# A two-layer graph network: second-layer matmuls in two column halves, and one-hots built tile by tile

## The chip, the cores and the metric

The kernel runs on one core of a Trainium2 chip. The metric is the device time of one execution in microseconds (us). The engines are named as the profile names them: PE is TensorE (PEld its weight loads), DVE is VectorE, ACT is ScalarE, POOL is GpSimd, SP is SyncE, which issues most of the DMAs.

## What is computed

6250 nodes and 200000 edges (sorted by target), 64 features, all float32. The reference, cut to what matters:

```python
h = relu(layernorm(x));  x = x + gcn_layer(h, src, dst)          # layer 0, untouched by the change
h = relu(layernorm(x))
message_in = concat(h[src], h[dst], edge_x)                      # 200000 x 192
message = relu(message_in @ msg_W1 + msg_b1) @ msg_W2 + msg_b2
agg = segment_sum(message, dst)
out = x + relu(concat(agg, h) @ upd_W1 + upd_b1) @ upd_W2 + upd_b2
```

## The kernel before

For the second layer `h @ W` is computed once per node for the source part (table `a`) and the target part (table `b`). What is left per edge is relu(a[src] + b[dst] + edge_x @ W_edge), summed by target. `msg_W2` is applied after the sum.

The edges are cut into 196 superblocks of 8 tiles of 128 edges. Since the edges are sorted, a superblock's targets lie in a window of 64 nodes. The tile `eo` holds per edge 64 values of `edge_x` and 64 of a one-hot of its target in that window; `wb` holds W_edge (64 rows) over the window's 64 rows of `b` (64 rows). So one matmul with 128 rows of contraction gives the edge term and the target term together, and the same one-hot serves later to sum messages into the window.

The loop (`message_passes` on DVE, the `Fori` over `passes1` on PE, here one pass) has 49 iterations of U = 4 superblocks, steps k = 0 to 3; the last two are written out. Per superblock:

- DVE `onehots_of` (through `window_onehots`, L905) compares `iota_w` with `rel` for 8 tiles in one instruction and writes the right half of `eo`. It runs three superblocks ahead.
- PE `transpose_edges` (L1692) turns 8 tiles of `eo` into PSUM, two superblocks ahead; ACT copies them to `eoT` (L1392).
- PE `edge_and_target_terms` (L1701): 8 matmuls with the stationary `eoT` tile (128x128) and the moving `wb` (128x64), one superblock ahead, into PSUM bank 2 or 3.
- DVE `add_rows` (L1137) adds the source rows and sets `added`; ACT applies `relu` (L1397); PE `sum_messages` (L1711) multiplies message tiles (128x64 stationary) with one-hots, even tiles into partitions 0 to 63, odd ones into 64 to 127; DVE `add_sums` (L1144) adds the result to `acc` at the window's base.

The source rows `a[src]` come in two ways. For 22 of the 32 tiles of an iteration POOL gathers them from DRAM (L684), one indirect DMA per tile, 8 for k = 0, 8 for k = 1, 6 for k = 3. For the other 10, in groups g = 0 and 1 of 5 tiles, PE picks them from a table held in SBUF. This path, per group:

- DVE `edges_to_slots` (L1093, L1094, L1096): a one-hot of the edge's bin (7 wide) times its source number, and a one-hot of its rank (128 wide), for 5 tiles each. The last instruction sets `ranked`. The first sets `bin_marked`, for which the third waits.
- PE `pack_slots` (L1726) waits for `ranked` and packs the source numbers into slots (5 matmuls); DVE `copy_packed` (L1101) copies them.
- PE `spread_slot_src` (L1737), ACT copy (L1405), DVE `picks` (L1109, 7 instructions of 896 elements), PE `pick_rows` (L1759, 49 matmuls, in four parts u), ACT copy (L1414).
- DVE `slots_to_edges` (L1118, 7 instructions of 640 elements), PE `return_rows` (L1773, 35 matmuls), DVE `build_rows` (L1127, three reduces).

Each engine works through an order written out by hand in `step`, and the engines meet only at semaphores:

- DVE, even k: `onehots_of` (k + 3), `add_rows` (k), `picks`, `build_rows`, `edges_to_slots` (one group on), `add_sums` (k). Odd k: `onehots_of`, `add_rows`, `copy_packed`, `slots_to_edges`, `add_sums`.
- PE, even k: `spread_slot_src`, transposes (k + 2), terms (k + 1), `return_rows`, `sum_messages` (k). Odd k: transposes, `pack_slots`, `pick_rows` u = 0 and 1, terms (k + 1), `pick_rows` u = 2 and 3, `sum_messages` (k).

An odd step's `pack_slots` thus uses the `edges_to_slots` of the even step before it. SP loads `edge_x` (two DMAs of 128 KB), source indices and the window of `b` for a superblock when `summed` and `added` of the one four before have come. POOL starts a superblock's gathers when its indices have landed (`idx_in`).

Of the kernel before, what the change touches and what calls it, by code (L numbers as in the profile page):

```python
# [20 lines left out]
def gnn_two_layers(nc: bass.Bass, x, src, dst, edge_x, l0_w, l0_b, msg_w1, msg_b1, msg_w2, msg_b2,  # L21
# [5 lines left out]
    N, D = x.shape  # L27
    E = src.shape[0]
    P = 128
# [3 lines left out]
    T = 8  # L33
    SB = T * P
    NSB = -(-E // SB)
    U = 4
# [4 lines left out]
    W = 64  # L41
# [26 lines left out]
    GTS = (5, 5)  # L68
    PT = sum(GTS)
    GOFF = (0, GTS[0])  # L70
# [6 lines left out]
    BINS = 7  # L77
# [22 lines left out]
    def wide(ap, axis, n):  # L100

        shape = list(ap.shape)
        shape[axis] = n
        return ap.broadcast_to(shape)

    ctx = ExitStack()
    with ctx:
        def sb(name, shape, dt=f32):
            return ctx.enter_context(nc.sbuf_tensor(name, shape, dt))

        def sem(name):
            return ctx.enter_context(nc.semaphore(name))
# [33 lines left out]
        pe_src, pe_bin, pe_rank, pe_slot, pe_far = (  # L146
            tmp_e[:, :, :].rearrange("p s t -> p (s t)").bitcast(fp16)[:, q * NPT:(q + 1) * NPT] for q in range(5))
# [44 lines left out]
        eo = work[:, 0:U * T * 2 * D].rearrange("p (u t d) -> p u t d", u=U, t=T)  # L192
        wb = sb("wb", [P, U, D])
        eoT = sb("eoT", [P, 2, T, P])
# [4 lines left out]
        digit16 = sb("digit16", [P, SLOTS_G], fp16)  # L199
# [44 lines left out]
        rank_oh = y_flat[:, 0:o].bitcast(fp16).rearrange("p (g t s) -> p g t s", g=2, t=GT)  # L244
        bin_src = y_flat[:, o:o + GT * BINS].bitcast(fp16).rearrange("p (g t b) -> p g t b", g=2, t=GT)
# [13 lines left out]
        psum = ctx.enter_context(nc.psum_tensor("psum", [P, 8, 512], f32))  # L259
# [63 lines left out]
        onehot = [sem(f"onehot{l}") for l in range(3)]  # L323
# [31 lines left out]
        s_tab3 = sem("s_tab3")  # L355
        s_split_v = sem("s_split_v")
        code_in = [sem("code_in0"), sem("code_in1")]
        bin_marked = sem("bin_marked")
        ranked = sem("ranked")
        packed = sem("packed")  # L360
        packed_copied = sem("packed_copied")
# [359 lines left out]
        def _(dve):  # L721
# [8 lines left out]
            V = nc.vector  # L730
# [8 lines left out]
            for c in range(0, CH, 4):  # L739
                m = min(4, CH - c)  # L740
# [24 lines left out]
            rel2 = rel[:, :, :].rearrange("p s t -> p (s t)")  # L765
# [11 lines left out]
            for c in range(0, CH, 4):  # L777
                m = min(4, CH - c)
                dve.wait_ge(s_tabT, (CH + 3) // 4 + c // 4 + 1)
                ins = V.tensor_copy(srci[:, c * P:(c + m) * P], psum[:, c // 4, 0:m * P])  # L780
# [56 lines left out]
            for g in range(CH):  # L837
                k = g % 2
# [65 lines left out]
            def window_onehots(s, out_slot):  # L904
                return V.tensor_tensor(out_slot, wide(iota_w.rearrange("p (t c) -> p t c", t=1), 1, T),  # L905
                                       wide(rel2[:, bass.ds(s * T, T)].rearrange("p (t c) -> p t c", c=1), 2, W), ALU.is_equal)
# [4 lines left out]
            for c in range(0, NB, 4):  # L911
                m = min(4, NB - c)
                dve.wait_ge(s_tr, c // 4 + 1)
                V.tensor_copy(hT[0:D, c * P:(c + m) * P], psum[0:D, (c // 4) % 2, 0:m * P]).then_inc(s_trc, 1)
            for c in range(0, NB, T):
                m = min(T, NB - c)
# [153 lines left out]
            def message_passes():  # L1070
                with dve.Fori(0, passes1) as r:

                    def onehots_of(i, k):
                        dve.wait_ge(summed[1], r * NSB + i * U + k + 1)
                        window_onehots(i * U + k, eo[:, k, :, D:2 * D]).then_inc(onehot[1], 1)

                    def pieces_of(i, g):
                        return NPIECE * (r * NIT + i) + (len(PIECES[0]) if g else 0)

                    def edges_to_slots(i, g, first=False):  # L1080
                        n = 2 * (r * NIT + i) + g
                        tiles = bass.ds(i * PT + GOFF[g], GTS[g])
                        if not first:
                            dve.wait_ge(packed, n - 1)
                        to_bin, to_rank = bin_src[:, g, 0:GTS[g], :], rank_oh[:, g, 0:GTS[g], :]

                        def each_edge(t, m):
                            return wide(t[:, tiles].rearrange("p (t c) -> p t c", c=1), 2, m)

                        def digits(m):  # L1090
                            return wide(digit16[:, 0:m].rearrange("p (t c) -> p t c", t=1), 1, GTS[g])

                        V.tensor_tensor(to_bin, digits(BINS), each_edge(pe_bin, BINS), ALU.is_equal).then_inc(bin_marked, 1)  # L1093
                        V.tensor_tensor(to_rank, digits(P), each_edge(pe_slot, P), ALU.is_equal)  # L1094
                        dve.wait_ge(bin_marked, n + 1)
                        V.tensor_tensor(to_bin, to_bin, each_edge(pe_src, BINS), ALU.mult).then_inc(ranked, 1)  # L1096

                    def copy_packed(i, g):
                        n = 2 * (r * NIT + i) + g
# [77 lines left out]
                    for k in range(1, 3):  # L1177
                        onehots_of(0, k)
# [117 lines left out]
            for c in range(0, NB, T):  # L1296
                m = min(T, NB - c)
# [153 lines left out]
        def _(pe):  # L1451
            TT = nc.tensor
# [12 lines left out]
            for c in range(0, NSB * T, 512):  # L1465
                m = min(512, NSB * T - c)
                ins = TT.matmul(psum[:, c // 512, 0:m], first_row[:, :], dstf[:, c:c + m], start=True, stop=True)
# [3 lines left out]
            for q in range(T):  # L1471
                ins = TT.matmul(psum[:, 5, 256 + q * CH:256 + (q + 1) * CH], expand[:, q, :], rawf[:, :, 0], start=True, stop=True)
# [8 lines left out]
            for half in range(2):  # L1481
                pe.wait_ge(s_edgeslot, half + 1)
                for b in range(NHALF):
                    col = 128 + half * NHALF + b
                    ins = TT.matmul(psum[:, 6, col:col + 1], edge_slot[:, b, :], ones_b[:, :], start=True, stop=True)
                ins.then_inc(s_slotcnt, 1)

            for g in range(CH):
                pe.wait_ge(s_slotoh, g + 1)
                for t in range(T):  # L1490
                    ins = TT.matmul(psum[:, 4, 0:HI], one_lo[:, g % 2, :, t], one_hi[:, g % 2, :, t],
                                    start=(g + t == 0), stop=(g + t == CH + T - 2))
                ins.then_inc(s_slothist, 1)

            with pe.If(passes > 1):
                TT.matmul(psum[:, 4, 0:HI], zeros[:, :], zeros[:, 0:HI], start=True, stop=False)
                pe.sem_inc(s_hfree, 2)
                with pe.Fori(0, NSB // 2) as i:
                    for k in range(2):
                        pe.wait_ge(s_oh, 2 * i + k + 1)  # L1500
                        for t in range(T):
                            ins = TT.matmul(psum[:, 4, 0:HI], one_lo[:, k, :, t], one_hi[:, k, :, t], start=False, stop=False)
# [21 lines left out]
            for b in range(NB):  # L1524
                c = b // 4
                if b % 4 == 0 and c >= 2:
                    pe.wait_ge(s_trc, c - 1)
                ins = TT.transpose(psum[0:D, c % 2, (b % 4) * P:(b % 4 + 1) * P], H[:, b + 1, :], ident[:, :])
# [4 lines left out]
            for b in range(NB):  # L1533
                c = b // T
                if b % T == 0 and c >= 2:
                    pe.wait_ge(s_mmc, c - 1)
                ins = TT.matmul(psum[:, 2 + c % 2, (b % T) * D:(b % T + 1) * D], hT[0:D, b * P:(b + 1) * P], w_l0[:, :],  # L1537
                                start=True, stop=True)
# [13 lines left out]
            for q in range(NCODE):  # L1552
                m = min(P, NPT - q * P)
                ins = TT.transpose(psum[0:m, 5, q * P:(q + 1) * P], code32[:, q * P:q * P + m], ident[:, :])
# [61 lines left out]
            with pe.If(passes > 1):  # L1616
                pe.sem_inc(summed[2], U)
                pe.sem_inc(acc_add[2], 2)
                with pe.Fori(0, passes) as r:
                    pe.wait_ge(counts_reset[2], r + 1)  # L1620
                    pe.sem_inc(s_turn[3], 1)
                    with pe.Fori(0, NIT) as i:
                        for k in range(U):
                            n = r * NSB + i * U + k
# [3 lines left out]
                            for t in range(T):  # L1628
                                ins = TT.matmul(psum[0:D, 6 + k % 2, 0:W], rows[:, k, t, :], onehot0[:, k, t, :],
                                                start=(t == 0), stop=(t == T - 1))  # L1630
# [3 lines left out]
            for b in range(NB):  # L1634
                c = b // T
                if b % T == 0 and c >= 4:
                    pe.wait_ge(s_gelu_in, c - 3)
                ins = TT.transpose(psum[:, c % 4, (b % T) * D:(b % T + 1) * D], acc[0:D, b * P:(b + 1) * P], ident[0:D, 0:D])
# [44 lines left out]
            with pe.Fori(0, passes1) as r:  # L1683
# [11 lines left out]
                def edge_and_target_terms(i, k):  # L1695
                    n = r * NSB + i * U + k
                    pe.wait_ge(b_in[k], 16 * (r * NIT + i + 1))
                    for t in range(T):
                        if t % 4 == 0:
                            pe.wait_ge(eoT_ready, 2 * n + t // 4 + 1)  # L1700
                        ins = TT.matmul(psum[:, 2 + k % 2, t * D:(t + 1) * D], eoT[:, k % 2, t, :], wb[:, k, :],  # L1701
                                        start=True, stop=True)
                    ins.then_inc(pre_done, 1)

                def sum_messages(i, k):
# [169 lines left out]
```

## Time and profile before

| | |
|---|---|
| time, three runs | 2358.78, 2360.42, 2361.4 us; median 2360.42 |
| profiled execution, its own time | 2360.0 us (its span) |
| instructions | 72737 |
| busy: PE, PEld, DVE, ACT, POOL | 2148.9, 1935.2, 1690.4, 1143.2, 1654.0 us |
| second layer's message loop | about 866 to 2320 us |
| L1701 (terms), PE busy | 374.4 us, 3136 records |
| L905 (one-hots, second layer), DVE busy | 135.6 us, 196 instructions |
| L1094 (rank one-hots), DVE busy | 80.1 us, 98 instructions |

How to read it: the page has the busy time of each engine and the same in 40 slices. A line of a timeline gives the start, the length, the engine, the source line and how many instructions were merged (x7); the idle time before it and what ended it stand in brackets. An instruction's length contains a tail that the next one overlaps, so the distance between starts is what one costs in a row. The chain of waits is followed back from the end of the program. "issue" is time in which the profile shows nothing that was waited for. A float32 matmul is recorded twice.

### The profile page before, as it was taken

To read this page: it belongs to the slowest core of one execution; us is meant where nothing else is said; L and a number is where in the kernel's file an instruction comes from. 1 tells how busy PE (TensorE), PEld (TensorE's weight loads), DVE (VectorE), ACT (ScalarE), POOL (GpSimd) and SP (SyncE) were. 2 spreads that over 40 slices of the span, in tenths; PEclk is the share of its full clock that TensorE was granted. 3 is DMA by queue.
4 is the path that set the end of the run, shared out by engine and by line. 5 is a ranking of instruction groups with operands and counts; after the bars stand their busy time and mean duration, and the time that the engine had idled before them with its cause. 6 is when DMAs were issued, how large, how long until landed. Compare 5 with 4: busy or idle time off the path is not lost.

```text
span 2360.0 us, 72737 instructions
## 1 busy us (share of the span) xinstructions
PE 2148.9 (91%) x23689; PEld 1935.2 (82%) x23690; DVE 1690.4 (72%) x4590; ACT 1143.2 (48%) x2411; POOL 1654.0 (70%) x1577
## 2 busy tenths in 40 slices
PE   2255999999999759999999999999999999999998
PEld 1143788887888659999999999999999999999995
DVE  8866788887888676666666666666666666666663
ACT  0003888888888644444444444444444444444442
POOL 5476777777777126777777777777777777777771
PEclk7566999999999879999999999999999999999999
DMA  2001111111112033333333333333333333333332
GB/s 74 1 1 42 26 27 27 27 27 29 27 25 28 6 86 65 73 74 74 74 74 74 74 74 74 74 74 74 74 74 74 74 74 74 74 74 74 74 75 41
DMA packets 346918, 133.36 MB, mean 57 GB/s; under 512 B 305501, under 2 KB 322755, under 8 KB 346787
## 3 DMA queue, kind: packets, MB, share of 16 engines
q1 hardware_dynamic: 298980, 82.66, 15.6%
q0 software_dynamic: 47808, 49.05, 11.1%
q8 instruction: 71, 1.16, 0.2%
q14 instruction: 59, 0.48, 0.1%
HBM read 124.04 MB, written 7.52 MB: 56 GB/s over the span
## 4 chain that ended last, share of the span: by engine, by line
PE 86%; DVE 7%; issue 3%; POOL 2%; ACT 1%; DMA 1%; DVEq 0%; SPq 0%; PEld 0%; POOLq 0%; PEldq 0%; ACTq 0%
PE psum L1759 17%; PE psum L1701 14%; PE psum L1570 12%; PE psum L1773 12%; PE psum L1602 9%; PE psum L1692 8%; PE psum L1711 5%; PE psum L1591 2%; PE psum L1737 2%; POOL rows L684 2%; PE psum L1726 1%; PE psum L1581 1%; PE psum L1537 1%; DVE work L830 1%; PE psum L1831 1%
## 5 line engine op out<-in xcount | busy, mean ns | idle before, releaser
L684 POOL DMA_INDIRECT rows<-a_rows,idx x1078 | 1110.4, 1030 | 378.9 <-issue 369.5
L1339 ACT ACTIVATE hT<-psum 128x392 bf16<-128x392 f32 x1152 | 510.6, 501 | 105.3 <-PE psum L1602 98.2
L684 POOL DMA_INDIRECT rows<-g_rows,idx x416 | 430.9, 1036 | 149.1 <-issue 125.7
L1570 PE MATMUL psum<-work,hT 128*128 128x192 bf16 x3528 | 455.0, 246 | 0.3 <-ACT hT L1339 0.3
L1759 PE MATMUL psum<-edge_index,H 128*128 128x192 bf16 x4802 | 429.2, 246 | 1.8 <-DVE H L1109 1.7
L1392 ACT ACTIVATE eoT<-psum 128x512 f32<-128x512 f32 x392 | 213.7, 602 | 404.9 <-PE psum L1692 404.8
L1759 PEld LDWEIGHTS psum<-edge_index,H 128*128 128x128 bf16 x4802 | 398.3, 99 | 3.4 <-issue 1.9
L1570 PEld LDWEIGHTS psum<-work,hT 128*128 128x128 bf16 x3528 | 323.5, 99 | 70.7 <-issue 1.0
L1602 PE MATMUL psum<-Z,one_lo 128*128 128x392 f16 x1152 | 364.8, 338 | 17.0 <-DVE Z L946 16.8
L1701 PE MATMUL psum<-wb,eoT 128*128 128x64 f32 x3136 | 374.4, 273 | 0.0
L1701 PEld LDWEIGHTS psum<-wb,eoT 128*128 128x128 f32 x3136 | 365.6, 192 | 0.1
L1414 ACT ACTIVATE Y<-psum 128x384 bf16<-128x384 f32 (+1 forms) x392 | 176.9, 451 | 365.5 <-PE psum L1759 357.0
L1773 PE MATMUL psum<-Y,Z 128*128 128x192 bf16 x3430 | 306.7, 246 | 0.9 <-ACT Y L1405 0.9
L946 DVE TENSOR_SCALAR Z<-digit,edge_index 128x392 f16<-128x392 f16 x1152 | 297.6, 328 | 0.0
L1773 PEld LDWEIGHTS psum<-Y,Z 128*128 128x128 bf16 x3430 | 294.7, 99 | 1.1 <-ACT Y L1405 1.1
L1109 DVE TENSOR_SCALAR H<-Y,node_cmp 128x896 bf16<-128x896 f16 x686 | 263.7, 452 | 7.5 <-ACT Y L1405 7.3
L1144 DVE TENSOR_TENSOR acc<-acc,psum 128x64 f32 x196 | 42.7, 218 | 311.0 <-PE psum L1711 311.0
L905 DVE TENSOR_TENSOR work<-iota_bw,rel 128x512 f32<-128x512 f32 x196 | 135.6, 692 | 118.5 <-issue 118.5
L1118 DVE TENSOR_SCALAR Z<-Z,slot_cmp 128x640 bf16<-128x640 f16 x686 | 220.2, 389 | 0.0
L1692 PE MATMUL psum<-ident,work 128*128 128x128 f32 x1568 | 212.0, 278 | 0.0
L1602 PEld LDWEIGHTS psum<-Z,one_lo 128*128 128x128 bf16 x1152 | 160.3, 145 | 38.5 <-DVE Z L946 27.9
L1692 PEld LDWEIGHTS psum<-ident,work 128*128 128x128 f32 x1568 | 168.7, 141 | 7.3
(272 smaller groups left out, 2012.6 us busy)
## 6 DMA issues: line engine op xcount, KB each, us to landing
work<-in_edge_attr_dram SPq DMA_DIRECT2D x392, 128.0 KB
rows<-a_rows,idx POOLq DMA_INDIRECT x1078
Z<-slot_code SPq DMA_DIRECT2D x98, 160.0 KB, 3.1
rows<-g_rows,idx POOLq DMA_INDIRECT x416
idx<-src_by_tile SPq DMA_DIRECT2D x200, 4.0 KB
wb<-b_rows SPq DMA_DIRECT2D x196, 16.0 KB
g_rows<-Y SPq DMA_DIRECT2D x1, 1600.0 KB, 8.9
a_rows<-Y SPq DMA_DIRECT2D x6, 256.0 KB, 2.6
```

Source lines behind the costliest of these rows:

```text
L684: pool.indirect_dma_start(out=rows[:, k, t, :], out_offset=None, in_=table, in_offset=bass.IndirectOffsetOnAxis(ap=idx[:, k, t:t + 1], axis=0)
L946: V.tensor_scalar(keys[:, g * T + t, :], key_digit[:, :], key_of[:, bass.ds(tile + t, 1)], None, ALU.is_equal).then_inc(key_ready, 1)
L1109: ins = V.tensor_scalar(pick[:, b, :], slot_src[:, :], node_cmp[:, b:b + 1], None, ALU.is_equal)
L1118: ins = V.tensor_scalar(from_slot[:, b, 0:cols], code_row[:, g, 0:cols], slot_cmp[:, b:b + 1], None, ALU.is_equal)
L1339: nc.scalar.activation(counts[:, j % 2, :, t * SLOTS:(t + 1) * SLOTS], psum[:, t % 4, 0:KEYS].rearrange("p (h m) -> p h m", m=SLOTS), ACT.Copy
L1392: nc.scalar.activation(eoT[:, k % 2, h * 4:h * 4 + 4, :], psum[:, h, :].rearrange("p (t e) -> p t e", e=P), ACT.Copy).then_inc(eoT_ready, 1)
L1570: ins = TT.matmul(psum[:, 4 + (j + 1) % 2, 0:NPART * D], counts[:, (j + 1) % 2, h, :], gtab[:, h, :, :].rearrange("p k d -> p (k d)"), sta ...
L1602: TT.matmul(psum[:, t % 4, 0:KEYS], one_lo[:, t // T, :, t % T], keys[:, t, :], start=True, stop=True).then_inc(counted, 1)
L1692: ins = TT.transpose(psum[:, h, (t % 4) * P:(t % 4 + 1) * P], eo[:, k, t, :], ident[:, :])
L1701: ins = TT.matmul(psum[:, 2 + k % 2, t * D:(t + 1) * D], eoT[:, k % 2, t, :], wb[:, k, :], start=True, stop=True)
L1759: ins = TT.matmul(psum[:, PICK_BANK[u], (b % 2) * NPART * D:(b % 2 + 1) * NPART * D], pick[:, h, b * P:(b + 1) * P], atab[:, b * BLK + h, ...
L1773: ins = TT.matmul(psum[:, bank, (t - t0) * NPART * D:(t - t0 + 1) * NPART * D], from_slot[:, b, t * P:(t + 1) * P], picked_rows[:, b, :], ...
```

## The change

- In `edge_and_target_terms` each tile's matmul becomes two, with the left and the right 64 columns of the stationary `eoT` tile (64 edges each), written to partitions 0 to 63 and 64 to 127 of the same PSUM columns. The moving operand is the same for both.
- In `onehots_of` of the second layer the one instruction for 8 tiles becomes 8 `tensor_scalar`, each comparing 64 float16 numbers (`digit16`) with the tile's column of `rel`, a per-partition scalar. The other uses of `window_onehots` stay.
- In `edges_to_slots` the three `tensor_tensor` for 5 tiles become 5 pairs of `tensor_scalar`: bin compared with `pe_bin` and multiplied with `pe_src` in one instruction, rank compared with `pe_slot`. The semaphore `bin_marked` and its wait go.

```diff
@@ DVE, onehots_of
-                        window_onehots(i * U + k, eo[:, k, :, D:2 * D]).then_inc(onehot[1], 1)
+                        for t in range(T):
+                            ins = V.tensor_scalar(eo[:, k, t, D:2 * D], digit16[:, 0:W], rel2[:, bass.ds((i * U + k) * T + t, 1)],
+                                                  None, ALU.is_equal)
+                        ins.then_inc(onehot[1], 1)
@@ DVE, edges_to_slots
-                        tiles = bass.ds(i * PT + GOFF[g], GTS[g])
                         if not first:
                             dve.wait_ge(packed, n - 1)
-                        to_bin, to_rank = bin_src[:, g, 0:GTS[g], :], rank_oh[:, g, 0:GTS[g], :]
...
-                        V.tensor_tensor(to_bin, digits(BINS), each_edge(pe_bin, BINS), ALU.is_equal).then_inc(bin_marked, 1)
-                        V.tensor_tensor(to_rank, digits(P), each_edge(pe_slot, P), ALU.is_equal)
-                        dve.wait_ge(bin_marked, n + 1)
-                        V.tensor_tensor(to_bin, to_bin, each_edge(pe_src, BINS), ALU.mult).then_inc(ranked, 1)
+                        for t in range(GTS[g]):
+                            at = bass.ds(i * PT + GOFF[g] + t, 1)
+                            V.tensor_scalar(bin_src[:, g, t, :], digit16[:, 0:BINS], pe_bin[:, at], pe_src[:, at],
+                                            ALU.is_equal, ALU.mult)
+                            ins = V.tensor_scalar(rank_oh[:, g, t, :], digit16[:, 0:P], pe_slot[:, at], None, ALU.is_equal)
+                        ins.then_inc(ranked, 1)
@@ PE, edge_and_target_terms
-                        ins = TT.matmul(psum[:, 2 + k % 2, t * D:(t + 1) * D], eoT[:, k % 2, t, :], wb[:, k, :],
-                                        start=True, stop=True)
+                        for half in (0, D):
+                            ins = TT.matmul(psum[half:half + D, 2 + k % 2, t * D:(t + 1) * D], eoT[:, k % 2, t, half:half + D],
+                                            wb[:, k, :], start=True, stop=True)
```

## Rows read from the trace of the kernel before

**Rows 1.** The page: busy time of the engines, share of the span, instructions.

```profile
PE 2148.9 (91%) x23689; PEld 1935.2 (82%) x23690; DVE 1690.4 (72%) x4590; ACT 1143.2 (48%) x2411; POOL 1654.0 (70%) x1577
```

**Rows 2.** By stretch: PE, PEld, DVE, ACT, POOL busy, granted clock, DMA share, GB/s.

```profile
0.00:250.00 250.00, 104.27 (x741) 79.10 (x743) 195.86 (x270) 39.61 (x94) 142.65 (x116) 0.65 0.12 29
...
1000.00:1500.00 500.00, 495.48 (x5986) 470.56 (x5985) 340.30 (x919) 203.92 (x409) 385.67 (x375) 1.00 0.35 74
```

**Rows 3.** Chain of waits, 1600 to 1630: start us, us, what.

```profile
1603.51 0.28 PE psum L1726 x5
...
1606.21 1.76 PE psum L1701 x16
...
1609.70 0.61 PE psum L1711 x16
...
1618.03 0.13 issue
1618.16 0.28 PE psum L1726 x5
```

**Rows 4.** Timeline of POOL: start us, us, engine, line [idle before].

```profile
1600.18 1.11 POOL L684 DMA_INDIRECT rows<-a_rows,idx  x1 [0.30 <-issue]
...
1608.18 0.94 POOL L684 DMA_INDIRECT rows<-a_rows,idx  x1 [0.30 <-issue]
...
1626.45 1.42 POOL L684 DMA_INDIRECT rows<-a_rows,idx  x1 [0.30 <-issue]
...
1629.60 1.12 POOL L684 DMA_INDIRECT rows<-a_rows,idx  x1 [0.30 <-issue]
```

**Rows 5.** Timeline of DVE, one half iteration, from its 1600 to 1620.

```profile
1601.79 0.56 DVE L1127 TENSOR_REDUCE rows<-psum 128x128 f32<-128x384 f32 x1 [0.21 <-PE psum L1773]
...
1610.46 0.22 DVE L1144 TENSOR_TENSOR acc<-acc,psum 128x64 f32 x1 [3.11 <-PE psum L1711]
1611.44 0.69 DVE L905 TENSOR_TENSOR work<-iota_bw,rel 128x512 f32<-128x512 f32 x1 [0.75 <-issue]
1612.05 0.68 DVE L1137 TENSOR_TENSOR msg<-psum,rows 128x512 f32<-128x512 f32 x1
1612.65 2.69 DVE L1109 TENSOR_SCALAR H<-Y,node_cmp 128x896 bf16<-128x896 f16 x7
1615.26 0.81 DVE L1127 TENSOR_REDUCE rows<-psum 128x64 f32<-128x192 f32 x2
1616.43 0.56 DVE L1127 TENSOR_REDUCE rows<-psum 128x128 f32<-128x384 f32 x1 [0.36 <-PE psum L1773]
1616.90 0.19 DVE L1093 TENSOR_TENSOR Y<-digit,tmp_e 128x35 f16<-128x35 f16 x1
1617.00 0.81 DVE L1094 TENSOR_TENSOR Y<-digit,tmp_e 128x640 f16<-128x640 f16 x1
1617.74 0.19 DVE L1096 TENSOR_TENSOR Y<-Y,tmp_e 128x35 f16<-128x35 f16 x1
...
1619.61 2.26 DVE L1118 TENSOR_SCALAR Z<-Z,slot_cmp 128x640 bf16<-128x640 f16 x7
```

**Rows 6.** Groups of the loop, 960 to 2300: weight loads of L1711.

```profile
L1711 PEld LDWEIGHTS psum<-work,msg 128*64 128x64 f32 x2912 | 99.6, 137 | 28.9 <-issue 28.9
```

**Rows 7.** Timeline of DVE in other stages: small instructions with scalars.

```profile
407.77 0.27 DVE L951 TENSOR_SCALAR slot_oh<-iota_bw,slot_node 128x128 f32<-128x128 f32 x1
407.97 0.36 DVE L953 TENSOR_REDUCE part<-psum 128x64 f32<-128x192 f32 x1
...
816.28 1.62 DVE L1223 SCALAR_TENSOR_TENSOR Z<-psum,dis,Y 128x64 f32<-128x64 f32 x8
...
2322.70 0.29 DVE L1059 TENSOR_SCALAR slot_cmp<-slot_cmp,rnd_step,rnd_cmp 128x7 f32<-128x7 f32 x1
2322.90 0.34 DVE L1060 TENSOR_SCALAR tmp_e<-tmp_e,rnd_rank 128x490 f16<-128x490 f16 x1
```

**Rows 8.** Timeline of ACT: the relu of the even step.

```profile
1612.77 0.63 ACT L1397 ACTIVATE msg<-msg 128x512 f32<-128x512 f32 x1
```

More of the change, by code:

```diff
@@ L357, in gnn_two_layers @@
         code_in = [sem("code_in0"), sem("code_in1")]
-        bin_marked = sem("bin_marked")
         ranked = sem("ranked")
@@ L1081, in edges_to_slots @@
                         n = 2 * (r * NIT + i) + g
-                        tiles = bass.ds(i * PT + GOFF[g], GTS[g])
                         if not first:
                             dve.wait_ge(packed, n - 1)
-                        to_bin, to_rank = bin_src[:, g, 0:GTS[g], :], rank_oh[:, g, 0:GTS[g], :]
[L1087 to L1091, printed above, removed]
-                        V.tensor_tensor(to_bin, digits(BINS), each_edge(pe_bin, BINS), ALU.is_equal).then_inc(bin_marked, 1)
-                        V.tensor_tensor(to_rank, digits(P), each_edge(pe_slot, P), ALU.is_equal)
-                        dve.wait_ge(bin_marked, n + 1)
-                        V.tensor_tensor(to_bin, to_bin, each_edge(pe_src, BINS), ALU.mult).then_inc(ranked, 1)
+                        for t in range(GTS[g]):
[4 more added lines that the diff above has]
+                        ins.then_inc(ranked, 1)
                     def copy_packed(i, g):
```

## The prediction

> **What bounds the kernel now.** The page comes first: TensorE (PE) is busy for 91% of the span, VectorE (DVE) for 72%, GpSimd (POOL) for 70% [rows 1]. The table by stretch says where the change can act: the second layer's loop runs from about 866 to 2320 us, and in any full stretch of it PE is busy 99% at granted clock 1.00, which is 2.4 GHz, and DVE 68% [rows 2]. All of the change lies there.
>
> A share is not yet a bound, so the chain of waits comes next [rows 3]. It runs along PE without a hole except for one: 0.13 us of "issue" before L1726, the packing matmuls (`pack_slots`). That place is at 1603.51 and again at 1618.16, so half an iteration (two superblocks) takes 14.65 us. A whole one takes 29.42 (22 gathers, from the one at 1600.18 to the one at 1629.60 [rows 4]), which leaves 14.77 for the other half. Why a hole there? `pack_slots` waits for `ranked`, set by the last instruction of `edges_to_slots` on DVE. In DVE's timeline [rows 5] that one, L1096, starts at 1617.74 and takes 0.19; PE starts 0.23 after its end. So DVE's string already arrives last there, by a tenth of a microsecond. The reader is to see a loop with two legs:
> - PE, from pack to the end of the odd step's `sum_messages`: 1603.51 to 1610.31 = **6.80** [rows 3].
> - DVE, in order [rows 5]: `add_sums` at 1610.46, the one-hots L905 at 1611.44, `add_rows` L1137 at 1612.05, seven picks L1109 at 1612.65, three reduces L1127 from 1615.26, `edges_to_slots` from 1616.90 to 1617.93; PE again at 1618.16. On this way the third reduce waits for PE's `return_rows`: it starts at 1616.43. Without a wait it would start 0.09 before its forerunner's end (1615.26 + 0.81), as the instruction behind it does, so at 1615.98. DVE has 0.45 us of slack in this half. In the other half the reduce idles 0.21 from that end, so the slack is 0.30.
>
> **The change, part by part.**
>
> *1. Terms in halves (L1701).* 8 matmuls of 128 stationary columns (16 records, two for each float32 one) stand in the chain for 1.76 us [rows 3]. They become 16 of 64 columns, left and right half in turn. `sum_messages` (L1711) has that very shape: float32, 128x64 stationary, 64 moving columns, halves in turn; its 16 records take 0.61 [rows 3]. Twice that is 1.22: **-0.54 us** per superblock. Bounds: before L1711's weight loads PE's loader idles 28.9 us in 182 superblocks, 0.16 each [rows 6], which could be a cost of going from whole to half and come once more; and nothing below 1.22. I take 1.22, as the chain shows no such hole. One of the two superblocks of each half has its terms in the PE leg. The other's are done while DVE is in its leg; they only make `return_rows` earlier still, so that the slack of 0.45 and 0.30 is DVE's to use.
>
> *2. One-hots of the target (L905).* One instruction of 512 elements, 0.61 from its start to the next one's [rows 5], becomes eight of 64 with a per-partition scalar. No row has this form exactly. Near it [rows 7]: L951, 128 float32 elements and such a scalar, 0.20 to the next start; L1223, eight of 64 elements with one, 1.62 less the overlap of 0.09, 0.191 each. The seven picks, 896 elements, take 2.61 to the next start, 0.373 each, and L1118 with 640 takes (2.26 - 0.09) / 7 = 0.310 [rows 5]. That is 0.25 ns per element and 0.15 us at no elements. So nearly all of a 64-element instruction is fixed cost. Bounds: 0.14, just under that intercept, and 0.20; I take 0.18, between it and L1223: 8 x 0.18 = 1.44, **+0.83**.
>
> *3. One-hots of slot and rank (`edges_to_slots`).* L1093, L1094 and L1096 take 1.03 from first start to last end [rows 5], with `bin_marked` and its wait in it. Now five pairs: 7 elements with two scalars, 128 with one. For the former there is L1059, 7 elements and two scalars: 0.20 to the next start [rows 7]; for the latter 0.18 again. 5 x 0.20 + 5 x 0.18 = 1.90, and 0.09 that the last lasts beyond its spacing: 1.99, **+0.96**. Bounds: ten of 0.14 (+0.46), or 0.26 and 0.20 if a second scalar adds 0.06 to L951 (+1.36).
>
> Weighed against a rule: the rows say a fixed 0.15 us or so for each small instruction with a scalar [rows 5, 7]. The Trainium skill ("VectorE: DVE Perf Modes", the section on the TRN2 errata) says that an instruction on SBUF pays a fixed latency whatever its size, so many small tiles pay it many times, which speaks against this change. Its table there (58 cycles and the elements over the mode) would make a 64-element one about 0.09 us, an estimate from that page; by it the strings would cost next to nothing and the sum would end below no change.
>
> *The sum.* Per half +0.83 + 0.96 - 0.54, less the slack: 0.80 in one, 0.95 in the other, 1.75 per iteration. Full halves, in which a pack waits for such a string: 47 x 2 + 1 = 95; 95 x 0.875 = **+83 us**. The opening pays a few small strings more, the last superblocks, which have no `edges_to_slots`, save some 4 x 0.54: together nothing. From the profiled execution, span 2360.0 (the only time given for it), this makes 2443. The median of the runs, 2360.42, is 0.4 above it, within their spread.
>
> *What moves at nothing.* In the even step `relu` starts at 1612.77, as `add_rows` ends (1612.73) [rows 5, 8]. It comes 0.83 later; it has until `sum_messages`, which follows the `return_rows` that the reduce awaits until 1616.43, and that comes 0.54 earlier: 3.0 us of cover after its 0.63, of which 1.4 goes. In the odd step `add_sums`, the next one-hots, `add_rows` (with `relu` behind it), `copy_packed` and `slots_to_edges` queue behind the string and come 1 to 2 us later; DVE idles 3.11 us before the L1144 at their end [rows 5]. Without that cover L905's +0.83 would count twice. SP's loads and POOL's gathers follow `added` and `summed`, so they take the loop's rate. Gathers never wait now: 0.30 us lie between them, 0.94 is one with DVE idle, 1.42 beside L905 and L1137 [rows 4]. Their floor is 22 x 1.24 = 27.3 us per iteration; they take 29.42.
>
> **The rivals.**
>
> *A. Small instructions are cheap: not slower.* L1093 (35 elements, no scalar) has the next start 0.10 behind it. The point from which this decides: the 18 small instructions may take what the old strings took, the 0.54 and the slack: 1.64 + 0.54 + 0.375 - 0.09 = 2.47, or 0.137 each. At 0.10 the loop of the two legs would be 0.67 shorter, 14.0 per half. But then the gathers bind: 14.7 if they stay as slow beside DVE as now, 13.65 at their floor. Between these, 14.4: 95 x 0.3 = 29 off, 2331, with 2298 and 2360 as its ends. For it: the small ones' own work is tens of nanoseconds. Against it: every row with a per-partition scalar is at 0.19 or more, and the intercept is 0.15. Chance 0.15 (faster 0.11, same 0.04). The page's table named above leads here.
>
> *B. The matmul halves do not overlap.* If a 64-column record costs 0.08, between L1711's 0.038 and the 0.11 of a whole one (1.76 / 16), the terms take 2.56, so 1.34 per half more than in the sum: 2443 + 127 = 2570. L1711's 0.61 speaks against it. 0.03.
>
> *C. The clock.* PE would be idle about 2.1 us in one piece before each pack, busy 13.4 of 15.6 us, or 86%. In the first 250 us, busy 42%, the granted clock is 0.65, so mostly the lower level, 1.2 GHz [rows 2]. If it fell in the loop, the 6.26 of the PE leg would double: 2443 + 95 x 6.26 = 3038. But 86% is far nearer to the 99% of now. 0.02.
>
> *D. The gathers bind after all.* One beside picks takes 1.12 [rows 4]. If all did, it were 22 x 1.42 = 31.2 per iteration, the same as 29.42 + 1.75. It gives 2443 too and is in the forecast.
>
> **How the numbers follow.** Forecast 0.80: 2443. Its bounds: all 18 at 0.14 gives +0.06 per half, 2365; all at their upper ends, and 0.15 for the change of shape, gives 1.59 per half, 2511. The range, 2365 to 2510, is these, and leaves out A (0.15) and B with C (0.05). A measurement of this kernel can tell about 0.2%, 5 us, from no change. Faster 0.11, same 0.04, slower 0.85.
>
> **What would show it.** Right: L1701 as 32 records in 1.2 us, its busy time down; the small instructions 0.18 to 0.20 apart; the chain of waits leaving PE before each L1726 and following DVE's string back to `add_sums`, with over half of the loop on DVE; no wait at the third reduce; 31.2 us per iteration; now and then a gather that waits for its indices. Wrong: a spacing under 0.137, PE as closed as before, a clock under 1.00, or terms of over 1.76. If a reduce still waits for `return_rows`, PE's even leg is longer than I have it and the sum is too high.

## The result, and the profile of the changed kernel

The changed kernel takes 2479.77 us (median of 4, 2476.41 to 2495.48), the kernel before beside it 2359.61: ratio 1.0519, 95% interval 1.0489 to 1.055. That is 120 us slower; 83 were forecast. The profiled execution has a span of 2479.0.

The page: busy time of the engines, then the granted clock in 40 slices.

```profile
PE 2104.7 (85%) x26825; PEld 1837.1 (74%) x26826; DVE 1887.1 (76%) x6648; ACT 1143.0 (46%) x2411; POOL 1652.6 (67%) x1577
...
PEclk6557999999999699999899999899999999989999
```

PE's share fell from 91% to 85% and DVE's rose from 72% to 76% [rows 1]. The loop is no longer closed on PE. DVE's timeline over one half iteration answers to [rows 5]; L1139, L1075, L1132, L1104 and L1122 are `add_sums`, the target one-hots, `add_rows`, the picks and the reduces, and L1088 with L1090 are the new slot and rank pairs:

```profile
1607.45 0.22 DVE L1139 TENSOR_TENSOR acc<-acc,psum 128x64 f32 x1 [4.02 <-PE psum L1707]
1608.44 1.39 DVE L1075 TENSOR_SCALAR work<-digit,rel 128x64 f32<-128x64 f16 x8 [0.77 <-issue]
1609.75 0.68 DVE L1132 TENSOR_TENSOR msg<-psum,rows 128x512 f32<-128x512 f32 x1
1610.35 2.62 DVE L1104 TENSOR_SCALAR H<-Y,node_cmp 128x896 bf16<-128x896 f16 x7
1612.88 1.28 DVE L1122 TENSOR_REDUCE rows<-psum 128x64 f32<-128x192 f32 x3
1614.08 0.28 DVE L1088 TENSOR_SCALAR Y<-digit,tmp_e 128x7 f16<-128x7 f16 x1
1614.27 0.25 DVE L1090 TENSOR_SCALAR Y<-digit,tmp_e 128x128 f16<-128x128 f16 x1
1614.43 0.29 DVE L1088 TENSOR_SCALAR Y<-digit,tmp_e 128x7 f16<-128x7 f16 x1
...
1615.69 0.24 DVE L1090 TENSOR_SCALAR Y<-digit,tmp_e 128x128 f16<-128x128 f16 x1
...
1622.55 0.22 DVE L1139 TENSOR_TENSOR acc<-acc,psum 128x64 f32 x1 [2.36 <-PE psum L1707]
1623.94 1.39 DVE L1075 TENSOR_SCALAR work<-digit,rel 128x64 f32<-128x64 f16 x8 [1.18 <-issue]
```

The eight one-hots take 1.31 us to the next start (1608.44 to 1609.75), 0.16 each, where 0.61 stood. The pairs run from 1614.08 to the end of the last at 1615.93: 1.85 where 1.03 stood. A pair is 0.35: 0.19 for 7 elements with two scalars, 0.16 for 128 elements with one. The three reduces (x3) no longer wait for PE. The chain of waits leaves PE before each L1722 (pack) and comes back at it, 0.24 after the string's end:

```profile
1616.17 0.28 PE psum L1722 x5
...
1618.86 1.08 PE psum L1697 x32
1619.94 1.84 PE psum L1755 x21
1621.78 0.64 PE psum L1707 x16
```

From 1616.17 the PE leg runs to 1622.42, the end of L1707: 6.25, of which the terms (L1697, 32 records) are 1.08 instead of 1.76 [rows 3]. The terms are 0.68 shorter, but the leg only 0.55 (it was 6.80): the part of `pick_rows` behind the terms takes 1.84 where the kernel before had

```profile
1607.97 1.73 PE psum L1759 x21
```

and L1707 takes 0.64 instead of 0.61. The groups of the loop, 960 to 2400:

```profile
L1697 PE MATMUL psum<-wb,eoT 128*64 128x64 f32 x5760 | 210.8, 227 | 0.0
...
L1722 PE MATMUL psum<-Y 128*128 128x7 f16 x450 | 25.2, 169 | 167.6 <-DVE Y L1090 154.0 <-issue 13.7
```

PE idles before the pack for 167.6 us in 90 cases. And there is one thing that the forecast gave almost no chance. PE's timeline through two halves, one long, one not:

```profile
1596.30 1.09 PE L1687 MATMUL psum<-ident,work 128*128 128x128 f32 x8
1599.41 0.28 PE L1722 MATMUL psum<-Y 128*128 128x7 f16 x5 [2.02 <-DVE Y L1090]
1599.64 4.12 PE L1755 MATMUL psum<-edge_index,H 128*128 128x192 bf16 x28
...
1613.37 1.09 PE L1687 MATMUL psum<-ident,work 128*128 128x128 f32 x8
1616.17 0.28 PE L1722 MATMUL psum<-Y 128*128 128x7 f16 x5 [1.70 <-DVE Y L1090]
1616.39 2.47 PE L1755 MATMUL psum<-edge_index,H 128*128 128x192 bf16 x28
```

Both times PE waited for the string (2.02 and 1.70 us). Behind the first wait the same 28 matmuls of `pick_rows` took 4.12 us, behind the second 2.47. The table by stretch says why: its last columns are the granted clock, the DMA share and GB/s.

```profile
1599.40:1602.90 3.50, 3.49 (x28) 3.33 (x29) 3.50 (x16) 0.49 (x1) 2.69 (x3) 0.57 0.16 33
1602.90:1606.40 3.50, 3.50 (x60) 3.26 (x58) 0.53 (x2) 1.27 (x3) 2.79 (x3) 0.94 0.14 28
1616.20:1619.70 3.50, 3.50 (x63) 3.34 (x65) 3.50 (x16) 1.30 (x3) 2.64 (x3) 1.00 0.16 33
```

In the 3.5 us behind the first pack the clock was granted at 0.57, so for 3.0 of the 3.5 us at the 1.2 GHz level; behind the second at 1.00, 2.4 GHz. Microsecond by microsecond:

```profile
1598.00:1599.00 1.00, 0.00 (x0) 0.00 (x0) 1.00 (x7) 0.08 (x1) 0.83 (x1) 1.00 0.99 227
...
1599.40:1600.40 1.00, 0.99 (x12) 0.96 (x13) 1.00 (x8) 0.00 (x0) 0.70 (x2) 0.76 0.16 33
1600.40:1601.40 1.00, 1.00 (x8) 0.95 (x7) 1.00 (x5) 0.00 (x0) 0.93 (x1) 0.50 0.22 49
...
1602.40:1603.40 1.00, 1.00 (x9) 0.96 (x7) 1.00 (x4) 0.00 (x0) 0.70 (x2) 0.53 0.03 4
1603.40:1604.40 1.00, 1.00 (x29) 0.84 (x28) 0.03 (x1) 0.60 (x2) 0.70 (x2) 1.00 0.14 29
```

The clock was at 1.00 while PE idled, fell some 0.5 us after PE had started again, and was back near 1603.4, 3.4 us later. Measured from pack to pack over the timeline (93 halves from the fifth on), 40 halves last 16.6 to 17.2 us and 53 last 15.1 or 15.5, with a mean of 15.33; before, all 93 lie around 14.71. The granted clock over the whole loop fits this half by half: it falls 40 times, for 3.4 us each, once at the start of each of the 40 long halves (from 0.1 us before the pack to 1.4 behind it) and never in one of the 53 others. At half the clock 3.4 us do the work of 1.7, and a long half is 1.6 us longer than a short one of its kind. So the 119 us of the profiled spans are two parts, 122 by this rounding: 93 x (15.33 - 14.71) = 58 for the legs, and 40 x 1.6 = 64 for the clock.

### The profile page after: what moved, and what is told of

Same layout as the page of the kernel before. It is cut to its first block, busy times and chain, and to the rows that moved or that the text cites. A ratio compares the mean times of both kernels' runs of the same rounds, so it can differ in the third digit from the quotient of the medians.

```text
span 2479.0 us, 83088 instructions
## 1 busy us (share of the span) xinstructions
PE 2104.7 (85%) x26825; PEld 1837.1 (74%) x26826; DVE 1887.1 (76%) x6648; ACT 1143.0 (46%) x2411; POOL 1652.6 (67%) x1577
## 4 chain that ended last, share of the span: by engine, by line
PE 59%; DVE 23%; issue 9%; DVEq 6%; POOL 1%; ACT 1%; DMA 0%; SPq 0%; PEld 0%; PEldq 0%; POOLq 0%; ACTq 0%
PE psum L1755 19%; PE psum L1565 12%; PE psum L1597 8%; DVE H L1104 8%; PE psum L1697 6%; PE psum L1707 3%; DVEq L1143 2%; DVE work L1075 2%; PE psum L1586 2%; DVE Y L1088 2%; DVE Y L1090 2%; DVE rows L1122 2%; PE psum L1687 1%; PE psum L1769 1%; PE psum L1722 1%
## 5 line engine op out<-in xcount | busy, mean ns | idle before, releaser
L683 POOL DMA_INDIRECT rows<-a_rows,idx x1078 | 1111.1, 1031 | 499.8 <-issue 351.7
L683 POOL DMA_INDIRECT rows<-g_rows,idx x416 | 429.4, 1032 | 149.8 <-issue 126.3
L1755 PE MATMUL psum<-edge_index,H 128*128 128x192 bf16 x4802 | 491.7, 266 | 2.2 <-DVE H L1104 2.2
L1755 PEld LDWEIGHTS psum<-edge_index,H 128*128 128x128 bf16 x4802 | 440.7, 106 | 17.2 <-issue 2.3
L1075 DVE TENSOR_SCALAR work<-digit,rel 128x64 f32<-128x64 f16 x1568 | 281.2, 274 | 92.6 <-issue 92.5
L1769 PEld LDWEIGHTS psum<-Y,Z 128*128 128x128 bf16 x3430 | 285.4, 98 | 7.7 <-ACT Y L1400 1.1
L1139 DVE TENSOR_TENSOR acc<-acc,psum 128x64 f32 x196 | 42.6, 217 | 290.1 <-PE psum L1707 290.1
L1104 DVE TENSOR_SCALAR H<-Y,node_cmp 128x896 bf16<-128x896 f16 x686 | 257.1, 446 | 4.4 <-ACT Y L1400 4.4
L1697 PE MATMUL psum<-wb,eoT 128*64 128x64 f32 x6272 | 229.2, 227 | 0.0
L1697 PEld LDWEIGHTS psum<-wb,eoT 128*64 128x64 f32 x6272 | 202.2, 140 | 34.2 <-issue 34.2
L1722 PE MATMUL psum<-Y 128*128 128x7 f16 x490 | 27.5, 169 | 184.0 <-DVE Y L1090 169.6
```

The lines of the kernel that those rows point to most:

```text
L683: pool.indirect_dma_start(out=rows[:, k, t, :], out_offset=None, in_=table, in_offset=bass.IndirectOffsetOnAxis(ap=idx[:, k, t:t + 1], axis=0)
L1075: ins = V.tensor_scalar(eo[:, k, t, D:2 * D], digit16[:, 0:W], rel2[:, bass.ds((i * U + k) * T + t, 1)], None, ALU.is_equal)
L1104: ins = V.tensor_scalar(pick[:, b, :], slot_src[:, :], node_cmp[:, b:b + 1], None, ALU.is_equal)
L1697: ins = TT.matmul(psum[half:half + D, 2 + k % 2, t * D:(t + 1) * D], eoT[:, k % 2, t, half:half + D], wb[:, k, :], start=True, stop=True)
L1755: ins = TT.matmul(psum[:, PICK_BANK[u], (b % 2) * NPART * D:(b % 2 + 1) * NPART * D], pick[:, h, b * P:(b + 1) * P], atab[:, b * BLK + h, ...
L1769: ins = TT.matmul(psum[:, bank, (t - t0) * NPART * D:(t - t0 + 1) * NPART * D], from_slot[:, b, t * P:(t + 1) * P], picked_rows[:, b, :], ...
```

## The experiments

Two conditions of the machine can't be mixed. Beside the eight runs of the last part below the kernel before took 3770 to 3830 us instead of 2360, and its relatives likewise. There PE's stream of instructions has holes in the middle of blocks of matmuls, as in this timeline of PE in the first run of the halves alone:

```profile
2013.97 1.02 PE L1712 MATMUL psum<-work,msg 128*64 128x64 f32 x16
2018.11 0.56 PE L1738 MATMUL psum<-ident,Y 128*128 128x128 f16 x7 [3.12 <-issue]
2018.51 1.16 PE L1692 MATMUL psum<-ident,work 128*128 128x128 f32 x5
2020.44 0.80 PE L1692 MATMUL psum<-ident,work 128*128 128x128 f32 x3 [0.77 <-issue]
```

The 3.12 us in front of L1738 are waited for nothing that the trace shows. What causes them is open; the granted clock is low there as well (0.81 from 1500 to 2000 in the third run of the halves alone, where the kernel before at 2360 has 1.00). Those runs are read by two things only: their ratio to the kernel before beside them, and the half iterations in which PE has no such hole. Some of these hold a fall of the clock as well and are longer for it, so the shortest are used. All are of one kind, the one that takes 14.76 in the kernel before.

### At 2360: the changed kernel and three relatives

The kernel before took 2360.03 (16 runs) beside all four.

**The changed kernel again**, no edit.

> The changed kernel itself, as the measure for the other three of this batch. In the batches since the blind comparison PE's instruction stream has holes (idle with 'issue' in the middle of a block of matmuls) and the kernel before takes 3770 to 3830 us, so what is read is the half iterations without such a hole: 15.1 and 15.5 us with the clock at 1.00 as in the first trace of it, 16.7 and 17.1 where the clock falls. If the machine is as in the blind comparison: 2480.

Measured: 2486.79 us, ratio 1.0536 (1.0472 to 1.06). 46 of 93 halves are long, the others have a mean of 15.32. The result holds. The number of long halves differs from run to run (40, 46), and again each long half has one fall of the clock and no other half has any. Six more falls are 10 us, and the two profiled executions lie 12 apart (2480.74 and 2492.53), so this is the likely reason why this kernel's runs spread by 19 to 32 us and those of the kernel before by 3 to 6.

**The changed kernel with PE's wait filled.**

```diff
                         pe.wait_ge(rows_built, pieces_of(i, 0) if g else pieces_of(i - 1, 1))
+                        for _ in range(3):
+                            TT.matmul(psum[:, 6, 0:320], ones[:, :], dstf[:, 0:320], start=True, stop=True)
+                    pe.wait_ge(ranked, n + 1)
```

The wait for `ranked` stood at the head of `pack_slots` before.

> The changed kernel with three long float32 matmuls of constants (128x128 by 320, some 1.6 us in all, few instructions) between PE's waits for rows_built and for ranked, so that PE works through most of the 1.7 to 2.0 us that it idles there. Theory of the clock: the long halves (16.7 and 17.1 us) are the 1.2 GHz level granted after that idle time; with the filling, hole-free halves are at 15.1 and 15.5 only and the granted clock in them is 1.00; on an undisturbed machine 2417 us. Rival, another cause: a good third of the hole-free halves stays 1.6 us long.

Measured: **2400.42 us**, ratio 1.0174 (1.0157 to 1.0191): 86 us less than the changed kernel beside it, by giving PE more to do. PE's timeline and, for this kernel and then for the changed one beside it, the table of the stretch from 1000 to 1500:

```profile
1592.28 1.09 PE L1687 MATMUL psum<-ident,work 128*128 128x128 f32 x8
1593.22 1.88 PE L1721 MATMUL psum<-dstf,ones 128*128 128x320 f32 x6
1595.00 0.28 PE L1724 MATMUL psum<-Y 128*128 128x7 f16 x5
1595.20 2.47 PE L1757 MATMUL psum<-edge_index,H 128*128 128x192 bf16 x28
```

```profile
1000.00:1500.00 500.00, 499.06 (x7079) 440.27 (x7077) 394.25 (x1588) 198.46 (x397) 389.97 (x362) 1.00 0.33 72
```

```profile
1000.00:1500.00 500.00, 441.89 (x6418) 401.71 (x6417) 372.08 (x1487) 184.46 (x370) 360.39 (x343) 0.94 0.30 67
```

The clock is granted at 1.00 instead of 0.94, none of the 93 halves is long, and each `pick_rows` behind a pack takes 2.47. The halves are 14.9 and 15.3 us, 0.2 shorter than the short ones of the changed kernel, because PE goes from the last filling matmul straight into the pack (no idle in front of L1724) instead of starting up 0.24 after the string. That is part of the 86 us too, some 93 x 0.2 = 19; the rest is the clock. 93 x (15.12 - 14.71) = 38 us, and 40 were measured. The theory of the clock stands; its rival is out.

**Halves and target one-hots** (e6_halves_and_target), the `edges_to_slots` of before.

```diff
-                        window_onehots(i * U + k, eo[:, k, :, D:2 * D]).then_inc(onehot[1], 1)
+                        for t in range(T):
+                            ins = V.tensor_scalar(eo[:, k, t, D:2 * D], digit16[:, 0:W], rel2[:, bass.ds((i * U + k) * T + t, 1)],
...
-                        ins = TT.matmul(psum[:, 2 + k % 2, t * D:(t + 1) * D], eoT[:, k % 2, t, :], wb[:, k, :],
+                        for half in (0, D):
```

> Matmul halves and target one-hots changed, slot and rank one-hots as before. Two legs, in halves without holes at clock 1.00: 13.85 (halves alone) + 0.70 = 14.55 us; PE idles 1.0 us before the pack. On an undisturbed machine 2360 - 0.2 x 95 = 2340.

Measured: 2361.72 us, ratio 1.0006 (0.9996 to 1.0015), no change. The undisturbed halves are 14.27 and 14.67 us, so 14.47 against the 14.55 of the legs. But the mean of all is 14.70: every few halves one is longer. The waits of the loop and the group of the gathers (1000 to 2200) say by what:

```profile
PE psum L1730 <- DVE Y L1099: 86.1, 81, 1.2
...
DVE msg L1140 <- DMA rows<-a_rows,idx: 46.3, 40, 2.8
```

```profile
L684 POOL DMA_INDIRECT rows<-a_rows,idx x897 | 928.5, 1035 | 273.4 <-issue 271.2 <-DMA idx<-src_by_tile 2.1
```

`add_rows` waits 46.3 us for gathered rows, which it never did before, while POOL waits for nothing: 897 gathers, 1035 ns each and 0.30 between them, 22 of them 29.4 us. A faster pair of legs ran into the gathers. This is the gathers' part of rival A, and it was missing from this expectation. One half of 93 is at 16.35, and it is no fall of the clock, which stays at 1.00 through the whole loop: `add_rows` waited 2.78 us for gathered rows in it.

```profile
1454.51 0.69 DVE L1140 TENSOR_TENSOR msg<-psum,rows 128x512 f32<-128x512 f32 x1 [2.78 <-DMA rows<-a_rows,idx]
```

**Halves and slot and rank one-hots**, the target one-hots of before.

```diff
-                        V.tensor_tensor(to_rank, digits(P), each_edge(pe_slot, P), ALU.is_equal)
...
+                        for t in range(GTS[g]):
+                            at = bass.ds(i * PT + GOFF[g] + t, 1)
...
-                        ins = TT.matmul(psum[:, 2 + k % 2, t * D:(t + 1) * D], eoT[:, k % 2, t, :], wb[:, k, :],
+                        for half in (0, D):
```

> Matmul halves and slot and rank one-hots changed, target one-hots as before. Two legs, in halves without holes at clock 1.00: 13.85 + 0.83 = 14.68 us; PE idles 1.2 us before the pack. On an undisturbed machine 2355. If the strings add, the changed kernel is this and the one before it together: 13.85 + 0.70 + 0.83 = 15.38, between its 15.1 and 15.5.

Measured: **2352.81 us**, ratio 0.9973 (0.9961 to 0.9984): faster than the kernel before by 7 us. Halves of 14.39 and 14.85, mean 14.62, where 14.68 was expected; clock 1.00; no wait for a gather.

```profile
L683 POOL DMA_INDIRECT rows<-a_rows,idx x904 | 892.9, 988 | 308.5 <-issue 263.2 <-DMA idx<-src_by_tile 45.3
```

The gathers take 988 ns instead of 1035 (halves and target) or 1032 (the kernel before, same stretch), and POOL now waits for its indices (45.3 us in this stretch). Why they are quicker is not shown. The long L1094 is gone, and in the kernel before the gathers beside L905, L1094 or L1137 are the slow ones, at 1.29 to 1.46 us (80 of 898; here 42 of 904 take over 1.2). But the changed kernel is rid of L1094 as well, and its gathers take 1031 in the same stretch: 40 of 829 take over 1.6 us, mostly beside the picks (L1104). Such gathers also occur in the filled kernel (76 of 873) and in halves and target (28 of 897), which share the short target one-hots, and neither in this kernel nor in the one before.

### The runs at 3770 to 3830

**The matmul halves alone** (e1_halves_only and its repeats), run three times.

```diff
-                        ins = TT.matmul(psum[:, 2 + k % 2, t * D:(t + 1) * D], eoT[:, k % 2, t, :], wb[:, k, :],
-                                        start=True, stop=True)
+                        for half in (0, D):
+                            ins = TT.matmul(psum[half:half + D, 2 + k % 2, t * D:(t + 1) * D], eoT[:, k % 2, t, half:half + D],
+                                            wb[:, k, :], start=True, stop=True)
```

> The kernel before with the matmul halves alone. Theory of the two legs (PE from pack to sum_messages, DVE from add_sums to the string, each half iteration their sum): the terms take 1.08 instead of 1.76 us, as measured in the changed kernel, so 0.68 less in the PE leg, and the slack of 0.375 in front of the third reduce is used up too: 1.05 less per half, 13.65 us, about 2260 us in all, PE's clock at 1.00. Rival, the gathers bind: 22 of them take 29.42 per iteration now and 27.3 at their floor, so the loop stops at some 28.5 and the time at 2300 to 2360, and then add_rows on DVE waits for a DMA, which it does nowhere before.

> The same kernel as e1_halves_only, sent out again for a comparison in which the kernel before is at 2360. Two legs: 13.65 to 13.85 us per half (13.85 is what undisturbed halves of the first trace showed), 95 x 0.9 = 85 less than before, 2275. Rival, the gathers bind: halves at 14.2 or more and 2310 to 2360, with waits for a DMA before add_rows.

> The kernel before with the matmul halves alone, on a machine that, it is hoped, runs the kernel before at 2360. Two legs alone: 13.85 us per half, 2275. Gathers: in e6_halves_and_target POOL never waited, its gathers took 1.34 us each with the gap, 29.4 per iteration, and DVE's add_rows waited 46 us for a DMA; the instructions of DVE that go with slow gathers (L905, L1137, L1094) are all here, and closer together. So the gathers bind: 22 x 1.33 or a little over = 29.2 to 29.5 per iteration, 2345 to 2362, against 2360; add_rows waits for a DMA by more than in e6, and PE idles in short pieces with the clock at 1.00.

Measured, in turn: 3736.86 us, ratio 0.9731 (0.9653 to 0.9808); 3730.57, 0.9771 (0.9744 to 0.9797); 3750.6, 0.9822 (0.9782 to 0.9861). Faster each time, in spite of 6272 more PE instructions. In the three traces the shortest halves without holes are 13.83 to 14.10 us. So the matmul halves save 0.7 to 0.9 us per half against the 14.76 of this kind where nothing else binds. The 13.65 of the first expectation took the whole 0.68 of the terms off; with the 0.55 by which the leg got shorter it is 14.71 - 0.55 - 0.375 = 13.79. What this kernel takes where the kernel before takes 2360 is open. The gathers of the two kernels above speak for little gain.

**Target one-hots alone.**

> The kernel before with the target one-hots alone as eight instructions. Two legs: the string takes 1.31 instead of 0.61 (as measured in the changed kernel), less 0.375 of slack: 0.33 per half, 31 us in all, 2391. PE then idles some 0.8 us before a pack. If the granted clock falls there already, it is more: each fall costs 1.6 us, so up to 2391 + 95 x 1.6. Rival, that work beside PE's leg hides the string: 2360.

Measured: 3843.09 us, ratio 1.0075 (1.0044 to 1.0105). The shortest halves without holes are 15.14 and 15.16, then 15.28 and 15.32; 15.04 was expected (14.71 + 0.33), with PE idle for 0.6 before the pack.

**Slot and rank one-hots alone.**

> The kernel before with the one-hots of slot and rank alone as ten instructions. Two legs: 1.86 instead of 1.03, less 0.375 of slack: 0.46 per half, 43 us in all, 2403, with the clock at 1.00. With falls of the clock up to 150 more.

Measured: 3819.29 us, ratio 1.001 (0.9979 to 1.0042): inconclusive. Of its eleven halves without holes seven are 17.15 to 17.17, and the shortest is 15.59 (15.17 expected). DVE's timeline in one of the long ones:

```profile
1413.10 0.82 DVE L1119 TENSOR_REDUCE rows<-psum 128x64 f32<-128x192 f32 x2
1415.39 0.56 DVE L1119 TENSOR_REDUCE rows<-psum 128x128 f32<-128x384 f32 x1 [1.47 <-PE psum L1765]
```

The third reduce starts after 1.47 us of idle time, though PE's last `return_rows` matmul had ended 1.36 before its start. The condition of the machine seems to reach DVE too, and these halves can't be used.

**Both kinds of one-hots, matmuls whole.**

> The kernel before with both strings of small instructions and the matmuls left whole. In the batch before this one the kernel before itself took 3809 us, so its four kernels could not be read by the sums; this one goes out alone. Two legs: +0.70 and +0.83 per half, less 0.375 of slack: 1.16, 110 us in all, 2470 with the clock at 1.00. PE idles some 1.5 us before each pack. If the granted clock falls as in the changed kernel (1.6 us in 4 of 10 halves), 60 more, 2530. Rival, that DVE's strings hide: 2360.

Measured: 3974.06 us, ratio 1.0407 (1.036 to 1.0453). Six halves without holes are 16.07 or 16.08, with 1.48 of idle PE before the pack; 14.71 + 1.16 = 15.87 was expected for the mean of the two kinds. One more is shorter, 15.66, in which PE idled 1.14. The changed kernel's halves of the like kind are 15.50: the matmul halves give back 0.58 of this.

**The changed kernel filled with 20 short matmuls** (e5_after_filled and its repeat).

```diff
+                        for _ in range(20):
+                            TT.matmul(psum[:, 6, 128:256], ident16[:, :], ident16[:, :], start=True, stop=True)
+                    pe.wait_ge(ranked, n + 1)
```

> The changed kernel, with 20 matmuls of constants (128x128, float16) issued by PE into unused columns of the pack's bank between its waits for rows_built and for ranked, in iterations 2 and up: PE is busy for about 1.5 of the 2.0 us that it idles there. Theory of the clock: in 40 of 95 halves the granted clock falls to 1.2 GHz behind that idle time, which costs 1.6 us each; with the filling it stays at 1.00, the halves are all 15.1 or 15.5 us, and the time is 2480 - 63 = 2417, though PE does more. Rival, the long halves come from something else (a late transfer, SBUF contention): long halves stay, 2480 or more.

> The same kernel as e5_after_filled, sent out again, since the kernel before took 3809 us beside the first one. Where the kernel before is at 2360: theory of the clock, 2417 us, granted clock 1.00 in the loop, no half over 15.6 us. Rival, another cause of the long halves: 2480 or more, long halves stay.

Measured: 3919.42 us, ratio 1.0271 (1.0216 to 1.0327), and 3885.87, ratio 1.0299 (1.0249 to 1.0349). Only one half in both traces is without a hole: 20 more matmuls with their weight loads in each half met the slow instruction stream. Nothing on the clock follows. The long filling above, three matmuls, was made for that reason.

## Why the prediction was right, and what it missed

- *Where it binds.* Right. In all kernels with a longer string PE waits before the pack, for `ranked`. The two legs and the slack of the third reduce gave 14.55 and 14.68 for two kernels that were measured at 14.47 and 14.62, and 13.85 + 0.70 + 0.83 = 15.38 for the changed one, at 15.33 with the clock at 1.00.
- *Step 1, the terms.* Right in kind, low in size for the terms: -0.68 instead of -0.54. I took twice L1711's 0.61; 32 records in one row take 1.08. But the matmuls behind them take 0.14 more (1.84 instead of 1.73, and 0.64 instead of 0.61), so that the PE leg lost 0.55. That this is the 0.54 of the forecast is luck: two errors that cancel.
- *Step 2, target one-hots.* +0.70 instead of +0.83: 0.16 each, near the intercept of 0.15 from the picks and not near L1223's 0.191. L1223 reads PSUM and is another form of instruction, the new ones read SBUF; whether this is the reason was not tried. The 0.09 estimated from the Trainium skill ("VectorE: DVE Perf Modes", the section on the TRN2 errata) was too low by far: 0.16 was measured.
- *Step 3, slot and rank.* +0.82 instead of +0.96, for the same reason: 0.16 for 128 elements with one scalar. The 7 elements with two took 0.19, as L1059 had it.
- *The sum of the legs.* With these, 0.70 + 0.82 - 0.55 - 0.375 = 0.60 per half; measured 0.62. Two small terms are not in it and cancel: the gap between `add_sums` and the one-hots is longer in every other half (1623.94 - 1622.55 = 1.39 where before had 1.26), and from the first pick to the first reduce it is 2.53 instead of 2.61. 58 us against my 83: the terms that I had too high are the two strings of one-hots, by 0.13 and 0.14.
- *Rival C, the clock.* This is the step that failed. I gave it 0.02, since "86% is far nearer to the 99% of now", and priced it as the whole PE leg at half speed in every half, 3038 us. A mean share says nothing on a 2 us piece of idle time: the clock fell behind 4 to 5 in 10 of such waits, for some 3.4 us, and cost 1.6 us each, 64 us in all. More than half of the slowdown is this. Why it fell behind some waits and not behind others is open. Forecast 2443, with my terms too high by 25 us and the clock's 64 missing: 2482, against 2480 measured. The direction held by the mechanism that I gave, the range in part by luck: its upper part was meant for slower one-hots and left the clock out. That 2443 came within 37 us is two errors of opposite sign.
- *The gathers.* Right as a floor (rival A): with the legs at 14.47 the loop ran at 14.70. In the changed kernel they wait for their indices, as forecast, here 3.27 us before one:

```profile
1622.26 0.94 POOL L683 DMA_INDIRECT rows<-a_rows,idx  x1 [0.30 <-issue]
1626.47 2.12 POOL L683 DMA_INDIRECT rows<-a_rows,idx  x1 [3.27 <-DMA idx<-src_by_tile]
```

- *What moves at nothing.* Right: no reduce waits for `return_rows`, and DVE still idles 2.36 us in the odd step (3.11 before). The 4.02 in the first line of its timeline above belong to a half in which PE's clock had fallen.

## What to carry to other kernels

When two engines take turns in a loop, add up the two legs from one timeline, with the slack of each wait in them: this gave the half iterations within 1% for kernels that did not exist yet, where the clock stayed at 1.00. Then ask what else runs beside them: in one of those kernels the gathers bound. Instructions with a per-partition scalar cost 0.16 us each here at 64 as at 128 elements (0.31 at 640), so one 512-element instruction should not be cut into eight on the leg that binds. And an added wait on PE costs its own length and perhaps a stretch at half clock behind it, so price both: at this place three useless matmuls were worth 86 us.

## What the runs showed of the hardware that was not expected

- The granted clock fell after 40 and 46 of 93 waits in two runs of the changed kernel. The waits in front of the long halves are 1.70 to 2.04 us, those in front of the others 1.69 to 2.04: the length of the wait does not say which it will be. The falls come in 2 to 5 halves in a row in the first run, 2 to 7 in the second. Where the waits were 0.98 to 1.41 us (halves and slots) or 0.86 to 1.21 with one of 1.41 (halves and target) the clock fell in none of 93 halves.
- 32 records of float32 matmuls with 64 columns, the two column halves in turn, took 1.08 us, where 16 records with 128 columns took 1.76: 0.034 against 0.11 each. 0.14 of these 0.68 us were lost again in the matmuls behind them.
- A gather's instruction on POOL took 1032 ns in the kernel before, 988 in halves and slots, 1035 in halves and target and 1031 in the changed kernel. Gathers of over 1.6 us occurred only in the kernels with the short target one-hots; by what is open.
